# Handing one stage's stream to the next without the trip through memory

## The chip, the cores and the metric

The kernel runs on one core of a Trainium2 chip. The core has five engines that run side by side and wait for each other on semaphores: TensorE (PE, matrix products), VectorE (DVE), ScalarE (ACT), GpSimd (POOL), and SyncE (SP), which issues the transfers here. The metric is the time of one execution in microseconds on the device; lower is better.

## The reference

One transformer block on a stream of 4 x 1024 x 256 float32 values. Modulation vectors come from a small product `c @ wmod` per batch (shift, scale and gate, twice).

1. The stream is normalised over its 256 channels, scaled and shifted; `q`, `k`, `v` are `tanh(x @ W + b)` with 16 heads of 64; causal softmax attention over 1024 tokens; `tanh(ctx @ Wo + bo)`, gated, is added to the stream. Call the sum x1.
2. x1 is normalised again over its channels, scaled and shifted. This feeds two layers. Each has a projection to queries, keys and values of 8 heads on a token-shifted stream, normalised queries and keys with a rotation by position, attention in windows of 128 tokens with one window back, an output product added to the stream, and then a layer norm and a gated GELU feed-forward part, also added.
3. The result is gated and added to x1.

## The kernel before

Tokens lie on the 128 partitions; a batch is 8 tiles of 128 tokens, and the stream of all batches is 32 tiles of 256 channels. Products in float32 accuracy are made of three products of high and low halves (`three_products`, lines 74 to 76), so every operand is split once: the high half by ACT or POOL, the low half as a difference, mostly by DVE. Each engine's program is written out by hand, in order, with counted semaphores; there is no planner.

`phase_modulation_and_attention` works through 4 batches of 8 pairs of heads. A pair (`it`) has 12 units of scores (128 keys by up to 512 queries, for two heads): PE makes scores, ACT takes the exponential (`exps`, L512), DVE splits it (`high_probs` L307, `low_probs` L312), PE multiplies by the values (L710 to L712). In the same pair PE makes the six projections of the next pair (`project`), ACT takes tanh, DVE splits them (`split_projection`, L296), and ACT and DVE split the weights of the pair after that (`split_weights`, L506 and L288). This is done in every pair, in the very last one too, whose next pair does not exist. A batch end follows (PE: L820 to L834): four products of 24 matmuls with `Wo`, each followed by ACT's tanh (L609) and DVE's gate (`gate_attended`, L470), transpositions back, and DVE's addition to the stream (`add_attended`, L477). At the ends of batches 0 and 1 the stream of batch 2 or 3 is also normalised and transposed into `hT`; at the ends of batches 2 and 3 it isn't, there being none. SP stores the sum to x1 in memory (L253) and waits until it has landed.

`phase_layers` is a block of its own: all engines meet before it. SP reads x1 back into `stream` (L1045), then issues the masks, the projection weights `a_raw` (L1050), the rotation tables `rope` (L1052) and their scales, and the layer's other weights. DVE takes statistics of each tile (L1346), the variance in six small steps (`variance_steps`), ACT a square root (L1197) and the normalised tile (L1200), DVE the scale (L1337) and POOL the shift (L1094; DVE for batch 0). Then ACT makes the high half of the projection weights (L1208), DVE multiplies the rotation tables by the scales (L1362) and makes the low half (L1367). PE's first work (`stream_T`, L1597) waits for that.

Then comes a loop over the two layers on every engine (`Fori(0, L)`). A layer begins with a prologue in which the first tiles are transposed, projected and rotated, and goes on with a loop over 32 tiles (attention) and one over 8 chunks (feed-forward). In the attention loop POOL splits the feed-forward weights. In the feed-forward loop it splits the next layer's projection weights (`split_attention_weights`) and then multiplies the rotation tables (L1187). SP reloads these at each layer's end, after the second layer too, for the first one again.

`phase_output` reads x1 once more, gates, adds and stores.

## Time and profile before

| | us |
|---|---|
| median of 3 runs | 2459.71 (2459.40 to 2462.36) |
| the profiled execution's own time | 2460.19 |
| its span, first to last instruction | 2458.4 |
| PE busy | 2292.2 (93%) |
| DVE busy | 1967.5 (80%) |
| ACT busy | 1543.5 (63%) |
| POOL busy | 632.3 (26%) |
| mean granted clock of PE | 0.973 |

### The profile page before, as it was taken

The page shows a single profiled execution, that of the slowest core. Times are in us where ns is not written, and L with a number is a line of the kernel's source. Part 1 is how long each engine was busy: PE and PEld are TensorE (multiplying, and loading weights), DVE is VectorE, ACT ScalarE, POOL GpSimd, SP SyncE. Part 2 cuts the span into 40 slices and gives each one's busy share as a digit, 9 for nine tenths or more (in the row PEclk, how much of TensorE's full clock was granted, in tenths as well). Part 3 has the DMA queues.
Part 4 walks back from the last instruction along what each step waited for, and adds up shares of the span by engine and source line. Part 5 has one row for each costly group of instructions (what it writes and reads, how often), then busy time and mean ns, then how long its engine had stood idle before and what let it go on. Part 6 is the DMA issues. An engine that isn't in the chain of part 4 may idle for free. (4 is left out here: it accounts for less than half of the span.)

```text
span 2458.4 us, 65008 instructions
## 1 busy us (share of the span) xinstructions
PE 2292.2 (93%) x21328; PEld 1759.6 (72%) x21328; DVE 1967.5 (80%) x4616; ACT 1543.5 (63%) x3024; POOL 632.3 (26%) x711
## 2 busy tenths in 40 slices
PE   6999999999999999089999998999899999997995
PEld 4767767777777777067777776888677777776884
DVE  6999799979987996668888887566688888885666
ACT  5777577757765775347677676344477777773442
POOL 1000000000000000245555554222455555552222
PEclk9999999999999999589999999999999999998998
DMA  4000100010001000500000000100100000001004
GB/s 137 20 19 13 59 20 13 29 49 13 13 13 49 13 19 6 186 1 1 9 0 9 0 9 2 53 0 0 47 0 6 2 9 0 9 0 53 0 0 136
DMA packets 70205, 62.44 MB, mean 25 GB/s; under 512 B 3972, under 2 KB 67196, under 8 KB 69760
## 3 DMA queue, kind: packets, MB, share of 16 engines
q1 hardware_dynamic: 70144, 61.66, 7.9%
q8 instruction: 35, 0.57, 0.1%
q14 instruction: 26, 0.21, 0.0%
HBM read 49.05 MB, written 8.40 MB: 23 GB/s over the span
## 5 line engine op out<-in xcount | busy, mean ns | idle before, releaser
L512 ACT ACTIVATE at_p<-at_ps_s,at_shift 128x1024 f32<-128x1024 f32 (+3 forms) x384 | 336.0, 900 | 84.9 <-PE at_ps_s L682 48.6
L312 DVE TENSOR_TENSOR at_p_lo<-at_p,at_p_hi 128x1024 f16<-128x1024 f32 (+3 forms) x384 | 357.2, 951 | 5.5
L1233 ACT ACTIVATE ly_probs<-ly_masked,ly_small,ly_rq 128x256 f32<-128x256 f32 x512 | 301.0, 592 | 9.6 <-DVE ly_small L1426 5.2
L1123 POOL TENSOR_TENSOR ly_rope_a<-ly_rope_a,ly_rope_t 128x512 f32<-128x512 f32 x132 | 168.9, 1279 | 271.4 <-DVE ly_rope_t L1394 271.4
L710 PE MATMUL at_ps_o<-at_v,at_p_hi 128*128 128x65 f16 x2304 | 237.7, 193 | 0.0
L711 PE MATMUL at_ps_o<-at_v,at_p_hi 128*128 128x64 f16 x2304 | 236.8, 194 | 0.0
L712 PE MATMUL at_ps_o<-at_v,at_p_lo 128*128 128x65 f16 x2304 | 235.7, 192 | 0.0
L710 PEld LDWEIGHTS at_ps_o<-at_v,at_p_hi 128*128 128x128 f16 x2304 | 210.6, 96 | 34.5 <-issue 25.8
L307 DVE CAST at_p_hi<-at_p 128x1024 f16<-128x1024 f32 (+3 forms) x384 | 206.7, 556 | 22.7 <-ACT at_p L512 14.2
L1241 ACT ACTIVATE ly_operands_plain<-ly_ps 128x512 f32<-128x512 f32 x256 | 152.5, 596 | 100.8 <-PE ly_ps L1639 100.8
L712 PEld LDWEIGHTS at_ps_o<-at_v,at_p_lo 128*128 128x128 f16 x2304 | 212.3, 99 | 0.0
L711 PEld LDWEIGHTS at_ps_o<-at_v,at_p_hi 128*128 128x128 f16 x2304 | 212.0, 97 | 0.0
L1423 DVE CUSTOM_DVE_ANT_0 ly_masked<-ly_ps,ly_mask 128x256 f32<-128x256 f32 x520 | 199.2, 420 | 5.9 <-PE ly_ps L1628 2.5
L74 PE MATMUL ly_ps<-ly_a_hi,ly_operands 128*128 128x512 f32 x408 | 180.3, 442 | 16.4 <-DVE ly_operands L1373 11.8
L518 ACT ACTIVATE at_stage<-at_ps_m,at_bias 128x512 f32<-128x512 f32 x198 | 135.9, 686 | 77.3 <-PE at_ps_m L76 72.3
L74 PE MATMUL at_ps_m<-at_hT,at_w_hi 128*128 128x512 f32 (+1 forms) x396 | 174.0, 439 | 6.7 <-DVE at_hT L362 3.0
L75 PE MATMUL ly_ps<-ly_a_lo,ly_operands 128*128 128x512 f32 x408 | 163.6, 401 | 0.0
L76 PE MATMUL ly_ps<-ly_a_hi,ly_operands 128*128 128x512 f32 x408 | 162.9, 399 | 0.0
L1639 PE MATMUL ly_ps<-ident,ly_probs 128*128 128x128 f32 x1024 | 161.2, 280 | 0.6
L76 PE MATMUL at_ps_m<-at_hT,at_w_lo 128*128 128x512 f32 (+1 forms) x396 | 157.1, 397 | 0.0
L75 PE MATMUL at_ps_m<-at_hT,at_w_hi 128*128 128x512 f32 (+1 forms) x396 | 156.3, 395 | 0.0
L1649 PE MATMUL ly_ps<-ly_operands_plain,ly_values 128*64 128x128 f32 x2048 | 154.2, 282 | 0.0
(233 smaller groups left out, 6247.7 us busy)
## 6 DMA issues: line engine op xcount, KB each, us to landing
ly_a_raw<-in_ffn_wqkv SPq DMA_DIRECT2D x3, 1536.0 KB, 6.3
at_w_raw<-in_Wv SPq DMA_DIRECT2D x34, 128.0 KB, 2.2
at_w_raw<-in_Wq SPq DMA_DIRECT2D x34, 128.0 KB, 2.3
at_w_raw<-in_Wk SPq DMA_DIRECT2D x34, 128.0 KB, 2.3
at_xio<-in_states SPq DMA_DIRECT2D x4, 1024.0 KB, 6.8
x<-at_xio SPq DMA_DIRECT2D x4, 1024.0 KB, 4.4
stream<-x SPq DMA_DIRECT2D x4, 1024.0 KB, 9.8
out_x<-x SPq DMA_DIRECT2D x4, 1024.0 KB, 9.5
```

What stands on the lines that cost most here:

```text
L74: pe.matmul(out, w_hi, x_hi, start=first, stop=False, skip_group_check=True)
L75: pe.matmul(out, w_hi, x_lo, start=False, stop=False, skip_group_check=True)
L76: return pe.matmul(out, w_lo, x_hi, start=False, stop=last, skip_group_check=True)
L307: dve.tensor_copy(p_hi[u % P_RING][:, :, off:], probs[u % P_RING][:, :, off:]).then_inc(p_hi_done, 1)
L312: dve.tensor_tensor(p_lo[u % P_RING][:, :, off:], probs[u % P_RING][:, :, off:], p_hi[u % P_RING][:, :, off:], ALU.subtract).then_inc(p_lo ...
L512: act.activation(probs[u % P_RING][:, :, off:], ps_s[u % 2][:, :, off:], ACT.Exp, bias=shift[:], scale=SCORE_SCALE).then_inc(exp_done, 1)
L710: pe.matmul(out, ph, ones_hi, start=(kt == 0 and t == 0), stop=False, skip_group_check=True)
L711: pe.matmul(out[:, 0:DH], ph, lo, start=False, stop=False, skip_group_check=True)
L712: step = pe.matmul(out, pl, ones_hi, start=False, stop=(kt == qc * CT + t), skip_group_check=True)
L1123: pool.tensor_tensor(ra[:, i, :], ra[:, i, :], rt[:, i, :], ALU.add).then_inc(s["add_done"], 1)
L1233: step = act.activation(pr[:, j % 2, h, :], sm[:, j % 2, h, :], ACT.Exp, bias=small[:, j % 2, 1, h:h + 1], scale=rq[:, par, 2 * j + h:2 * ...
L1423: dve.tensor_tensor_reduce(sm[:, j % 2, h, :], ps_s[h][:, half], mask[:, par].rearrange("p a b -> p (a b)"), 1.0, -3.0e38, ALU.add, ALU.ma ...
```

## The change

- `stream`, the layers' input, is allocated in the memory of `hT`, the transposed stream of the attention stage. Its first half is `hT`'s half for even batches, free once batch 2's projections are made. The attention stage's query and key buffers share memory with the projection weights `a_raw` and `a_lo`.
- During the attention stage SP reads x1 of batches 0 and 1 back before the end of batch 2, and of batch 2 before the end of batch 3 (`load_attended`). At these batch ends DVE, POOL and ACT do the second norm of those batches with scale and shift (`second_statistics`, `second_shifts`, `second_normal`, `second_scale`, `second_offset`). Batch 3's sum is written straight into `stream` and stored from there; the attention block doesn't wait for that store any more, the layers block does where it writes over it.
- SP issues layer 0's `a_raw` after the last scores of the attention stage.
- Batch 3's norm stands inside layer 0's prologue (`last_statistics`, `last_variance`, `last_shifts`, `last_affine`), ahead of the attention loop. The rotation tables' products (`scale_rotations`) stand behind the first tile's low half. The square root becomes a power on POOL.
- The last pair of the attention stage makes no projections, values, weights or scores for a next one, and the last but one splits no weights.
- The layers are written out one after the other in place of the loop; what the second would prepare for a third is left out (the reload, the split of the projection weights, the rotation tables).

```diff
-        hT = a.sb("at_hT", [P, 2, 2, KT, S], F32R)
+        hT, stream, st_x, a_raw = (keep[n] for n in ("hT", "stream", "st_x1", "a_raw"))
...
+                def load_attended(b):
+                    sp.dma_start(stream[:, b * TB:(b + 1) * TB, :],
+                                 scr["x1"][b].rearrange("(t p) d -> p t d", p=P)).then_inc(ld_s[b], 16)
...
+                    ahead = HP if b + 2 < B else HP - 1 if b + 1 < B else HP - 2
+                    with sp.Fori(0, ahead) as j:
 
                         hold(sp, tick, (wh_done, at(b * HP + j + 2)), (wl_done, at(b * HP + j + 2)))
                         load_w(b * HP + j + 2)
                     if b + 2 < B:
...
+                    elif b + 1 < B:
+                        sp.wait_ge(pj_mm, at(NPJ * HP * (b + 1)))
+                        for i in range(b):
+                            load_attended(i)
+                        sp.wait_ge(wh_done, at(b * HP + HP + 1))
+                        sp.wait_ge(wl_done, at(b * HP + HP + 1))
+                        load_w(b * HP + HP + 1)
+                    else:
+                        sp.wait_ge(pj_mm, at(NPJ * HP * (b + 1)))
+                        load_attended(b - 1)
+                        sp.wait_ge(sc_done, NU * NPAIR)
+                        sp.dma_start(a_raw[:].rearrange("p (k n) -> p k n", k=KT),
+                                     io["ffn_wqkv"][0].rearrange("(k p) n -> p k n", p=P)).then_inc(keep["ld_a"], 16)
 
                     hold(sp, tick, (x1_done, at(NC * (b + 1))))
-                    sp.dma_start(scr["x1"][b].rearrange("(t p) d -> p t d", p=P), xio[:]).then_inc(st_x, 16)
-
-                    hold(sp, tick, (st_x, 16 * b + 16))
+                    src = xio[:] if b + 1 < B else stream[:, b * TB:(b + 1) * TB, :]
+                    sp.dma_start(scr["x1"][b].rearrange("(t p) d -> p t d", p=P), src).then_inc(st_x, 16)
+
+                    if b + 1 < B:
+                        hold(sp, tick, (st_x, 16 * b + 16))
...
+                for b in range(B - 1):
+                    tiles = slice(b * TB, (b + 1) * TB)
+                    pool.wait_ge(n2_var, b + 1)
+                    pool.tensor_tensor(col[:, 2, tiles], col[:, 1, tiles], expo[:], ALU.pow).then_inc(n2_rstd, 1)
...
+                def second_statistics(b):
+
+                    tiles = slice(b * TB, (b + 1) * TB)
+                    dve.wait_ge(ld_s[b], 16)
+                    for t in range(b * TB, (b + 1) * TB):
+                        dve.bn_stats(stats[:, t, :], stream[:, t, :]).then_inc(n2_bn, 1)
+                    dve.wait_ge(n2_bn, TB * (b + 1))
+                    variance_steps(dve, n2_chain, 5 * b, stats[:, tiles], col[:, 0, tiles], vtmp[:, :, tiles], col[:, 1, tiles], n2_var)
+
+                def second_shifts(b):
+                    tiles = slice(b * TB, (b + 1) * TB)
+                    dve.wait_ge(n2_rstd, b + 1)
+                    dve.scalar_tensor_tensor(col[:, 3, tiles], col[:, 0, tiles], -0.5, col[:, 2, tiles], ALU.mult,
+                                             ALU.mult).then_inc(n2_col, 1)
+
+                def second_scale(b):
+                    part = stream[:, b * TB:(b + 1) * TB, :]
+                    dve.wait_ge(st_rows, 16 * (B + 1))
+                    dve.wait_ge(n2_xn, b + 1)
+                    dve.tensor_tensor(part, part, modB[:, b, D:2 * D].unsqueeze(1).broadcast_to([P, TB, D]),
+                                      ALU.mult).then_inc(n2_scaled, 1)
+
+                def second_offset(b):
+                    part = stream[:, b * TB:(b + 1) * TB, :]
+                    dve.wait_ge(n2_scaled, b + 1)
+                    dve.tensor_tensor(part, part, modB[:, b, 0:D].unsqueeze(1).broadcast_to([P, TB, D]),
+                                      ALU.add).then_inc(n2_done, 1)
...
+                        if ahead_of:
+                            split_projection(ahead, 0, dst)
...
+                        if ahead_of > 1:
+                            split_weights(it + 2)
...
+                    with dve.Fori(0, HP // 2 - (0 if b + 1 < B else 1)) as j:
                         for par in range(2):
...
+                            pair(j * 2 + par, par)
+                    if b + 1 == B:
+                        pair(HP - 2, 0, 1)
+                        pair(HP - 1, 1, 0)
...
+                        into = xio[:, tiles, :] if b + 1 < B else stream[:, b * TB + c * CT:b * TB + (c + 1) * CT, :]
+                        dve.tensor_tensor(into, xio[:, tiles, :],
                                           (ps_s[1], ps_o)[c][:].rearrange("p h (t d) -> p (h t) d", d=D), ALU.add).then_inc(x1_done, 1)
 
+                    if b + 2 >= B:
+                        second_statistics(0 if b + 1 < B else b - 1)
+                    if b + 2 == B:
+                        second_statistics(1)
+                        second_shifts(0)
...
+                        second_shifts(1)
+                        second_scale(0)
+                        second_offset(0)
+                        gate_attended(0, 1)
+                        second_scale(1)
+                        gate_attended(1, 0)
+                        add_attended(0)
+                        second_offset(1)
                     else:
+                        second_shifts(b - 1)
+                        second_scale(b - 1)
                         gate_attended(0, 1)
+                        second_offset(b - 1)
...
+                def second_normal(b):
+
+                    act.wait_ge(n2_col, b + 1)
+                    for t in range(b * TB, (b + 1) * TB):
+                        step = act.activation(stream[:, t, :], stream[:, t, :], ACT.Identity, scale=col[:, 2, t:t + 1],
+                                              bias=col[:, 3, t:t + 1])
+                    step.then_inc(n2_xn, 1)
...
+                            if m == 0 and c == 0 and b + 2 >= B:
+                                second_normal(0 if b + 1 < B else b - 1)
+                            if m == 1 and c == 0 and b + 2 == B:
+                                second_normal(1)
...
+                load_attention(0)
+                sp.sem_inc(s["ld_attn"], 16)
                 sp.dma_start(prev_mask[:], io["prev_mask"]).then_inc(s["ld_const"], 16)
                 sp.dma_start(mask[:], io["mask"]).then_inc(s["ld_const"], 16)
...
+                    if l + 1 < L:
+                        hold(sp, s["tick"], (s["qkv_mm"], at(3 * (NT + 2) * (l + 1))))
+                        hold(sp, s["tick"], (s["ra_done"], at(6 * (NT + 1) * (l + 1))))
+                        load_attention(l + 1)
...
+                        pool.wait_ge(n0_var, 1)
+                        pool.tensor_tensor(col0[:, 2, :], col0[:, 1, :], expo[:], ALU.pow).then_inc(n0_rstd, 1)
...
+                        act.wait_ge(n0_col, 1)
+                        act.wait_ge(keep["st_x1"], 16 * B)
+                        for t in range(TB):
+                            step = act.activation(x[:, NT - TB + t, :], x[:, NT - TB + t, :], ACT.Identity,
+                                                  scale=col0[:, 2, t:t + 1], bias=col0[:, 3, t:t + 1])
+                        step.then_inc(n0_xn, 1)
...
+                def last_statistics():
+                    for t in range(TB):
+                        dve.bn_stats(st0[:, t, :], x[:, NT - TB + t, :]).then_inc(n0_bn, 1)
+
+                def last_variance():
+                    dve.wait_ge(n0_bn, TB)
+                    variance_steps(dve, n0_chain, 0, st0, col0[:, 0, :], tmp0, col0[:, 1, :], n0_var)
+
+                def last_shifts():
+                    dve.wait_ge(n0_rstd, 1)
+                    dve.scalar_tensor_tensor(col0[:, 3, :], col0[:, 0, :], -0.5, col0[:, 2, :], ALU.mult, ALU.mult).then_inc(n0_col, 1)
+
+                def last_affine():
+                    sb, cb = (modB[:, B - 1, i * D:(i + 1) * D].unsqueeze(1).broadcast_to([P, TB, D]) for i in range(2))
+                    dve.wait_ge(n0_xn, 1)
+                    dve.tensor_tensor(x[:, last, :], x[:, last, :], cb, ALU.mult).then_inc(n0_scaled, 1)
+                    dve.wait_ge(n0_scaled, 1)
+                    dve.tensor_tensor(x[:, last, :], x[:, last, :], sb, ALU.add).then_inc(n0_done, 1)
+
+                def scale_rotations():
+                    dve.wait_ge(s["ld_attn"], 48)
+                    for i in range(4):
+                        dve.tensor_tensor(rope[:, i], rope[:, i], rows[:, i, :].unsqueeze(1).broadcast_to([P, TB, DH]),
+                                          ALU.mult).then_inc(s["rope_q"], 1)
+                    after(dve, "rope_q", 4)
...
-                with dve.Fori(0, L) as l:
+                for l in range(L):
                     after(dve, "f_lo", nth_norm(l, 0))
                     stream_lo(l, 0, 0)
                     after(dve, "rope_next", 4 * l)
+                    if l == 0:
+                        scale_rotations()
+                        last_statistics()
                     squared_norms(l, 0, 1)
                     squared_norms(l, 0, 0)
                     rotate_q(l, 0, 0)
                     stream_lo(l, 1, 1)
+                    if l == 0:
+                        last_variance()
                     normalise_keys(l, 0)
                     rotate_k(l, 0, 0)
+                    if l == 0:
+                        last_shifts()
                     squared_norms(l, 1, 1)
                     copy_keys(l, 0, 0)
                     squared_norms(l, 1, 0)
                     stream_lo(l, 2, 0)
+                    if l == 0:
+                        dve.wait_ge(s["ld_const"], 32)
                     after(dve, "msk", (NT // 2 + 1) * l)
                     dve.tensor_copy(mask[:, 0, 1, :], prev_mask[:, 0, :]).then_inc(s["msk"], 1)
                     after(dve, "msk", (NT // 2 + 1) * l + 1)
                     maxima(l, 0, nth(l, 0), 0, 0)
                     maxima(l, 0, nth(l, 0), 1, 0)
+                    if l == 0:
+                        last_affine()
...
+        keep["stream"] = a.sb("stream", [P, NT, D])
+        with ExitStack() as shared:
+            keep["qk"] = [Allocator(nc, shared).sb(f"at_{n}{part}", [P, S], F16)
+                          for n in ("q0", "k0", "q1") for part in ("hi", "lo")]
+        with ExitStack() as shared:
+            keep["a_lo"] = Allocator(nc, shared).sb("ly_a_lo", [P, KT * 3 * INNER], F32R)
+        keep["a_raw"] = a.sb("ly_a_raw", [P, KT * 3 * INNER])
         phase_modulation_and_attention(nc, io, scr, keep)
-        keep["stream"] = a.sb("stream", [P, NT, D])
...
```

## Rows read from the trace of the kernel before

**Rows 1.** The page, 40 equal slices of the span: busy tenths of PE and DVE.
```profile
PE   6999999999999999089999998999899999997995
...
DVE  6999799979987996668888887566688888885666
```

**Rows 2.** Table of stretches: start:end, length, busy us (instructions) by engine, PEclk, DMA, GB/s.
```profile
939.20:965.20 26.00, 25.02 (x358) 18.02 (x357) 24.71 (x38) 19.09 (x27) 0.00 (x0) 1.00 0.04 11
...
990.00:1000.00 10.00, 0.07 (x1) 0.00 (x0) 1.22 (x1) 1.28 (x1) 1.17 (x7) 0.69 0.52 173
...
1030.00:1050.00 20.00, 0.68 (x2) 0.29 (x2) 15.29 (x7) 5.75 (x8) 12.00 (x7) 0.50 0.00 1
...
1048.00:1076.00 28.00, 19.48 (x73) 13.82 (x71) 13.97 (x37) 9.12 (x22) 13.16 (x16) 0.75 0.00 1
```

**Rows 3.** Timeline of the hand-over: start, us busy, engine, line, operation [idle before <-releaser].
```profile
990.11 1.22 DVE L477 TENSOR_TENSOR at_xio<-at_xio,at_ps_o 128x1024 f32<-128x1024 f32 x1 [1.19 <-PE at_ps_o L729]
991.42 0.37 SPq L253 DMA_DIRECT2D x<-at_xio  x1
996.33 5.73 SPq L1045 DMA_DIRECT2D stream<-x  x4
...
998.16 0.52 POOL L1089 MEMSET ly_values<- 128x512 f32 x1
1002.07 2.71 DVE L1346 BATCH_NORM_STATS2 ly_masked<-stream 128x6 f32<-128x256 f32 x8 [10.75 <-DMA stream<-x]
...
1005.39 0.17 DVE L89 SCALAR_TENSOR_TENSOR ly_masked<-ly_masked 128x8 f32<-128x8 f32 x1
...
1010.76 2.28 DVE L1337 TENSOR_TENSOR stream<-stream,modB 128x2048 f32<-128x2048 f32 x1
1010.88 4.04 ACT L1200 ACTIVATE stream<-stream,ly_masked 128x256 f32<-128x256 f32 x8 [0.47 <-DVE ly_masked L1352]
...
1031.59 2.84 ACT L1208 ACTIVATE ly_a_hi<-ly_a_raw 128x1536 fp32r<-128x1536 f32 x2
1031.71 4.84 DVE L1337 TENSOR_TENSOR stream<-stream,modB 128x2048 f32<-128x2048 f32 x1 [1.91 <-ACT stream L1200]
1036.47 6.99 DVE L1362 TENSOR_TENSOR ly_rope<-ly_rope,ly_rows 128x512 f32<-128x512 f32 x4
...
1043.39 3.62 DVE L1367 TENSOR_TENSOR ly_a_lo<-ly_a_raw,ly_a_hi 128x1536 fp32r<-128x1536 f32 x2
...
1047.70 0.68 PE L1597 MATMUL ly_ps<-ident,ly_xs 128*128 128x128 f32 x2 [57.64 <-DVE ly_a_lo L1367]
1048.66 1.28 ACT L1214 ACT_TABLE_LOAD   x1 [14.23 <-PE ly_ps L1597]
```

**Rows 4.** Timeline of the block change from the layers to the output, DVE and SP.
```profile
2430.08 1.29 DVE L1584 TENSOR_TENSOR stream<-stream,ly_ps 128x512 f32 x2 [0.54 <-PE ly_ps L1704]
...
2431.64 5.43 SPq L852 DMA_DIRECT2D out_x<-x  x4
```

**Rows 5.** DVE's timeline in the last pair.
```profile
943.40 1.28 DVE L296 TENSOR_TENSOR at_vT_lo<-at_stage,at_vT_hi 128x512 f16<-128x512 f32 x2
...
962.49 0.95 DVE L288 TENSOR_TENSOR at_w_lo<-at_w_raw,at_w_hi 128x768 fp32r<-128x768 f32 x1
```

**Rows 6.** DVE's timeline at the end of batch 2: the first two gates.
```profile
736.07 0.49 DVE L470 TENSOR_SCALAR at_y<-at_y,modT 128x512 f32<-128x512 f32 x1 [5.54 <-ACT at_y L609]
741.67 0.49 DVE L470 TENSOR_SCALAR at_y<-at_y,modT 128x512 f32<-128x512 f32 x1 [5.11 <-ACT at_y L609]
```

**Rows 7.** Timeline of layer 0's prologue and the first tile of its loop.
```profile
1064.15 1.28 POOL L1123 TENSOR_TENSOR ly_rope_a<-ly_rope_a,ly_rope_t 128x512 f32<-128x512 f32 x1 [0.46 <-DVE ly_rope_t L1394]
...
1068.04 1.65 POOL L1119 TENSOR_TENSOR ly_rk<-ly_norm,ly_expo 128x8 f32<-128x8 f32 x1 [2.61 <-DVE ly_norm L1382]
...
1072.75 0.69 DVE L1391 TENSOR_TENSOR ly_rope_a<-ly_ps,ly_rope 128x512 f32<-128x512 f32 x1
...
1078.56 0.48 PE L74 MATMUL ly_ps<-ly_a_hi,ly_operands 128*128 128x512 f32 x1
```

More of the change, by code:

```diff
@@ L604, in _ @@
+                    with act.Fori(0, HP // 2 - (0 if b + 1 < B else 1)) as j:
+                        for par in range(2):
+                            pair(j * 2 + par, par)
+                    if b + 1 == B:
+                        pair(HP - 2, 0, 1)
+                        pair(HP - 1, 1, 0)
                     for c in range(NC):
@@ L1144, in split_attention_weights @@
                     pool.tensor_tensor(a_lo[:, cols], a_raw[:, cols], f32(a_hi[:, cols]), ALU.subtract).then_inc(s["aw_done"], 1)
-                with pool.Fori(0, L) as l:
+                for l in range(L):
                     hold(pool, s["tick"], (s["ya_done"], at(NCH * l)))
@@ L1273, in u_high @@
                     act.activation(uT[rows_of, 0, i, :], uf[rows_of, i % 2, :], ACT.Copy).then_inc(s["u_hi"], 1)
-                with act.Fori(0, L) as l:
+                for l in range(L):
                     after(act, "y_mm", HT * NCH * l)
@@ L1712, in _ @@
                 after(pe, "w_lo_done", 2)
-                with pe.Fori(0, L) as l:
+                for l in range(L):
                     after(pe, "ya_done", NCH * l)
```

356 lines of the change are left out of this document (174 added, 182 removed).

## The prediction

> **What bounds the kernel now.** I read the page first: the slices of TensorE (PE) read nine almost everywhere, and zero in one, the seventeenth [rows 1]. That slice is where the attention stage hands over to the layers. The table of stretches gives its size: from 990 to 1000 us PE does one instruction, from 1030 to 1050 two, while VectorE (DVE) is busy 15.3 of 20 us, and the granted clock has fallen from 1.00 to 0.50 [rows 2]. So the kernel is bound by PE in its steady parts and by a chain of other engines in this gap. The timeline then gives that chain [rows 3]. DVE's last addition of the attention stage runs from 990.11 to 991.33. The result is stored (issue at 991.42), and the stream is read back by four transfers from 996.33. Statistics begin at 1002.07. For each of four batches DVE, ScalarE (ACT) and GpSimd (POOL) normalise, scale and shift in turn, and after that come the rotation tables (1036.47) and the low half of the projection weights (1043.39 to 1047.01). PE starts at 1047.70. From 991.33 to 1047.70 are 56.4 us with no matmul. Nothing else in the kernel is a bubble of this kind, apart from the last stage, which the change leaves as it is.
>
> **The change, part by part.** The sum is made against the profiled execution: span 2458.4 us, its own time 2460.2 us, which is 0.5 above the median 2459.7 of the runs shown.
>
> *The gap.* In the new kernel batches 0 to 2 arrive normalised, batch 3 is normalised later, the projection weights are in place, and the attention block no longer waits for its last store. What stays between DVE's last addition and PE's first transposition is:
> - the block change. Where nothing is stored it is short: the layers' last addition ends at 2431.37 and the next block's first transfer is issued at 2431.64 [rows 4]. I take 0.6 us, since the store's issue (0.37) now stands before SP's end: the new block starts at 991.9.
> - the start. The block began by 996.25 and POOL's last memset ended at 998.68 [rows 3], so 2.4 us: 994.3. A table load of ACT (1.28) fits under it.
> - the high half of the weights on ACT, 2.84 for two pieces, and behind its second piece one low half on DVE, 1.8 (half of 3.62) [rows 3]: 994.3 + 2.84 + 1.8 = 998.9, and 0.1 for the waits.
> PE therefore starts at 999.0 instead of 1047.7: **-48.7 us**. Bounds: -50.0 if the block starts at once and the pieces overlap better, -44 if the weights or the block end wait for something (the old wait for the store, 4.4 us, is the largest that stood here).
> The weight load is issued after the last scores, some 35 us before the end of the stage, into their memory. It is not on the path. The rotation tables are: they land behind the last store (1 MB) and are wanted only after the first low half of the stream, about 2 us after PE's start, 9 us after their issue. I take no wait, with 3 us as the upper bound.
>
> *The last pair without a next one.* The pairs are held by DVE, busy 24.7 of 26 us in the last one [rows 2]. The last pair drops six splits of projections (0.64 each, 1.28 for two), one copy of values of about the same size (0.6) and the split of weights (0.95, which overlaps to 0.86) [rows 5]: 5.3 us of DVE. PE, busy 25.0 of the 26, drops the 36 matmuls of six projections and more, and ACT, busy 19.1, drops twelve tanh, so neither takes over. Not all of it comes back, because at the end of the pair the context must pass PE and ACT before DVE can take its low half, and this stood behind the dropped split. I take **-4.5 us**, between -2 (PE and ACT latencies laid bare) and -6.6 (all of DVE's dropped work in both last pairs and its idle time).
>
> *Second norms inside the batch ends.* At a batch end without a next stream PE has four products of 24 matmuls, 5.6 us apart, and DVE idles for 5.5 and 5.1 us before its first two gates [rows 6]. Per batch come 2.71 (statistics), 0.74 (variance), and 2.28 twice (scale and shift); ACT gets 4.04, POOL a power of 1.65 [rows 3, 7]. At the end of batch 2 two batches are done. From DVE's end of the pairs on: statistics to 6.9, first shift column 7.1, gate 7.5, ACT's normals 7.2 to 11.3, scale and offset to 15.9, second gate 16.4. The first gate began 5.54 after DVE's pairs had ended (730.5), and the next 5.6 later [rows 6]; so the third product is done about 16.0 after that end, and there PE wants the second gate. That is **+0.5 us** (0 to +2). At the end of batch 3 only one batch is done, and its second gate comes at 13.2: nothing.
>
> *Layer 0's prologue.* It gains DVE work: four products of the rotation tables, 0.7 each where POOL is quiet (6.99 for four with POOL busy), statistics 2.71, variance 0.74, and before the loop the two operations on batch 3 (4.57). The first two fall before ACT's first square, about 7 us after DVE's first low half, and are hidden. The variance sits before the keys are normalised, +0.7. POOL's power of 1.65 comes before the second addition of the rotated keys, which began at 1064.15 [rows 7]: with the 0.7 it starts at 1065.4 on the old scale, +1.3 for everything behind. Then ACT normalises eight tiles (4.04), DVE scales and shifts: DVE's first rotation of the loop moves from 1072.75 to 1078.9. PE is not that late: its second projection of the loop, which waits for the keys, moves from 1078.56 to 1081.0 [rows 7]. From there on all is shifted by **+2.4 us**. Bounds: 0 if the steady part, where DVE's slices read eight [rows 1], gives it back, and +9.6 (0.7 + 1.65 + 4.04 + 2.28 and 0.9 for the clock, which read 0.75 in this stretch [rows 2]) if it stands on the path in full.
> The Trainium skill speaks against this step (SBUF — State Buffer, the section "SBUF: two separate sides"): DVE and GpSimd share a port pair as an exclusive lock, held for a whole instruction. The trace agrees: DVE's product on a whole batch took 2.28 us alone and 4.84 beside POOL's addition [rows 3]. By that rule the two operations before the loop would cost up to 5 us more, a sum of 2413.6. I leave it out because POOL here waits for them and has only short work.
>
> *The table load.* ACT loads a table at 1048.66, on the path between PE's first transposition and the copy of it, after the square root earlier in the block [rows 3]. The change computes no square root there: **-1.3 us** (0 if the load stays).
>
> *Layers unrolled; the reload at the end dropped.* The matmuls, waits and shapes inside the loops are the same. The second layer's useless weight split and its four products on POOL go, beside a PE whose slices read nine [rows 1]: 0. Waits whose value depended on the layer become constants: 0, bounds -3 to +3, since PE's slices read nine with that register work in its program.
>
> Sum: -48.7 - 4.5 + 0.5 + 2.4 - 1.3 = -51.6, so 2460.2 - 51.6 = 2408.6 us.
>
> **The rivals.**
> - *The prologue pays in full.* The work taken out of the gap comes back behind PE's restart: DVE's products wait for the tables (+3), its operations run beside POOL's, the power, normals and scaling stand on the path, and PE goes in and out of half clock as it does in this stretch now [rows 2]. For it: DVE is the busiest engine there, and its first operation of the loop does move by 6 us. Against: PE needs only the keys' part of it. Time: 2460.2 - 48.7 - 3 + 1 + 9.6 + 1 = 2420.
> - *More comes back.* The last pair gives all of DVE's dropped work (-6.6), the prologue costs nothing since the loop has slack, the register work shrinks (-3): 2460.2 - 50 - 6.6 - 1.3 - 1 = 2401.
> - *The other side: slower code in the unrolled layers.* The layers are now laid out twice, with new wait values and fresh code for the second layer at every loop entry. If a tile of the layers' attention (about 14 us, 64 of them) became 0.9 us longer, that is 58 us, and the kernel would end above 2465. It takes the whole gain back from 0.8 us a tile (51.6 / 64). For it: PE has no slack in that part. Against: the operations are the same, and the first layer's fresh code does not show as idle time in the slices now [rows 1].
> - *The gap stays in part:* the attention block ends late, since the last store or the weights hold it. 4.4 us: 2413. It is inside the range.
>
> **How the numbers follow.** Forecast 2408.5, chance 0.70 (2404 to 2414). Prologue in full 0.13, more comes back 0.13, slower code 0.02, and 0.02 for anything that holds the layers' start for nearly as long as now. The range that leaves out 2 in 10 is 2401 to 2419. A measurement of this kernel tells 0.2% (5 us) from nothing; all cases but the last two are far beyond it: faster 0.96, same 0.015, slower 0.025.
>
> **What would show it.** PE's idle stretch at the hand-over falls from 56.4 to about 8 us; the last pair lasts about 21.5 us instead of 26; PE's second projection of layer 0's loop begins about 32 us after its first transposition (30.9 now); no table load after that transposition; the stretches of the layers' loops are as long as now. The forecast is wrong if the gap is above 15 us, if a tile in the layers takes more than 14.3 us, or if DVE's two operations on batch 3 hold PE for more than 5 us.

## The result and the profile after

The changed kernel takes 2426.3 us (median of 4 runs, 2423.5 to 2427.0) against 2460.4 (median of 4, 2459.4 to 2462.4): a ratio of 0.9855, 95% interval 0.9843 to 0.9867. That is 34 us less, where 51 were forecast, and outside the range (2401 to 2419). The gap closed as forecast, and most of what is missing was lost in a place that the prediction had put at 0: in layer 1's attention loop ACT loads a table in every iteration.

I cut the spans at marks that both kernels have: the issues of the four stores of x1, PE's first transposition of the layers, and each layer's first and last addition of attended values on DVE. Times in us; the further columns are experiments told below.

| from, to | before | changed | exp once | last pair only | additions on DVE | all |
|---|---|---|---|---|---|---|
| start, first store | 285.38 | 286.96 | 286.60 | 286.49 | 285.56 | 285.73 |
| batch 1 | 236.67 | 237.20 | 237.19 | 236.76 | 237.17 | 237.17 |
| batch 2 | 235.07 | 235.60 | 235.55 | 235.25 | 235.60 | 235.60 |
| batch 3 | 234.29 | 231.45 | 231.43 | 229.38 | 229.85 | 229.84 |
| last store, PE's restart | 56.29 | 8.31 | 8.31 | 55.85 | 8.31 | 5.36 |
| restart, first addition | 30.89 | 31.79 | 31.61 | 30.34 | 31.75 | 33.53 |
| layer 0's loop | 450.73 | 449.70 | 449.75 | 450.99 | 449.73 | 450.96 |
| to layer 1's first addition | 241.18 | 238.05 | 237.85 | 241.23 | 237.97 | 237.99 |
| layer 1's loop | 450.72 | **466.88** | 450.30 | 450.98 | 450.24 | 450.25 |
| to the end | 237.16 | 239.25 | 236.01 | 236.62 | 235.67 | 235.62 |
| span | 2458.39 | 2425.18 | 2404.59 | 2453.89 | 2401.84 | 2402.04 |

The page of the changed kernel, the slices of PE and DVE. The zero of [rows 1], the seventeenth, is now a six. Nothing here betrays the loss in layer 1 (the 29th to the 36th slice): an engine that waits 1 us in 29 doesn't move a tenth.

```profile
PE   6999999999999999699999997999899999998994
...
DVE  6999799979998998688888886666788888885666
```

The table of stretches around the hand-over answers to [rows 2] (start:end, length, busy us and instructions by engine, PEclk, DMA share, GB/s). The first row covers the last pair. From DVE's last context product of the pair before (L352) to its own last one it now takes 23.6 us, against 26.1 in the kernel before; its granted clock is no longer 1.00.

```profile
941.00:965.00 24.00, 18.30 (x303) 12.35 (x302) 20.01 (x31) 11.61 (x15) 0.00 (x0) 0.93 0.21 78
...
990.00:1000.00 10.00, 0.49 (x2) 0.29 (x2) 4.54 (x3) 2.85 (x2) 2.95 (x12) 0.62 0.75 222
1000.00:1020.00 20.00, 15.29 (x57) 11.21 (x56) 14.75 (x38) 5.44 (x14) 11.31 (x11) 0.76 0.47 172
```

The timeline of the hand-over answers to [rows 3]. Read it as one chain: the last addition ends at 991.11, the store is issued, the new block's first transfer comes at 992.00, POOL's last memset ends at 994.36, ACT starts its high halves behind it, DVE's two low halves run one after the other to 999.41, and PE transposes at 999.51. ACT's copy of that comes without a table load.

```profile
989.89 1.22 DVE L547 TENSOR_TENSOR stream<-at_xio,at_ps_o 128x1024 f32<-128x1024 f32 x1 [1.19 <-PE at_ps_o L848]
991.20 0.37 SPq L276 DMA_DIRECT2D x<-stream  x1
992.00 0.35 SPq L1181 DMA_DIRECT2D ly_rope<-in_rope  x1
...
993.84 0.52 POOL L1222 MEMSET ly_values<- 128x512 f32 x1
994.39 2.85 ACT L1330 ACTIVATE ly_a_hi<-ly_a_raw 128x1536 fp32r<-128x1536 f32 x2 [6.21 <-POOL ly_values L1222]
...
995.98 3.43 DVE L1491 TENSOR_TENSOR ly_a_lo<-ly_a_raw,ly_a_hi 128x1536 fp32r<-128x1536 f32 x2 [4.87 <-ACT ly_a_hi L1330]
...
999.51 0.66 PE L1731 MATMUL ly_ps<-ident,ly_xs 128*128 128x128 f32 x2 [9.65 <-DVE ly_a_lo L1491]
1000.35 0.28 ACT L1336 ACTIVATE ly_operands<-ly_ps 128x128 fp32r<-128x128 f32 x1 [3.11 <-issue]
```

Now the lost part. ACT's groups by line name the table loads of the whole changed kernel: 16 of them stand at L1355, the exponential inside the attention loop.

```profile
L1355 ACT ACT_TABLE_LOAD x16 | 20.5, 1283 | 3.3 <-DVE ly_small L1549 2.4 <-issue 0.7
...
L1439 ACT ACT_TABLE_LOAD x2 | 2.6, 1283 | 5.9 <-PE ly_ps L1800 5.9
...
L649 ACT ACT_TABLE_LOAD x1 | 1.3, 1283 | 1.3 <-PEq L1993 1.3
```

The same view of the kernel before has six loads in all, none in a loop over tiles; two of them are at the first copy of a layer:

```profile
L1214 ACT ACT_TABLE_LOAD x2 | 2.6, 1283 | 19.4 <-PE ly_ps L1597 19.4
```

ACT's timeline at the head of one iteration in layer 1: the load, and 0.02 us after it the exponential that needed it. The next is at 1801.62, 29.3 us on, and so through the loop; an iteration is two tiles.

```profile
1771.72 0.60 ACT L1367 ACTIVATE ly_operands_plain<-ly_ps 128x512 f32<-128x512 f32 x1 [2.19 <-PE ly_ps L1793]
1772.33 1.28 ACT L1355 ACT_TABLE_LOAD   x1
1773.63 0.60 ACT L1355 ACTIVATE ly_probs<-ly_masked,ly_small,ly_rq 128x256 f32<-128x256 f32 x1
```

And PE's waits (us in total, times, longest). First layer 1's loop in the changed kernel, 1719 to 2186, then layer 0's, 1031 to 1481, where the exponential's table is still active from the attention stage and nothing is loaded. In the kernel before, PE waits in layer 1's loop (1771 to 2221) only once, for 1.6 us.

```profile
PE ly_ps L1773 <- ACT ly_probs L1355: 15.7, 15, 1.2
PE ly_ps L1800 <- DVE ly_operands_plain L1565: 1.6, 1, 1.6
```

```profile
PE ly_ps L1800 <- DVE ly_operands_plain L1565: 1.6, 1, 1.6
PE ly_ps L1773 <- ACT ly_operands_plain L1363: 0.2, 1, 0.2
```

This is how I read it. A load is placed where an instruction needs a table that may not be active. In the rolled loop over the layers the first copy of a layer got one, since the code before it can be the entry or the previous layer's Gelu, and the exponential loop inherited it. Unrolled, the prologue of layer 1 holds only copies and squares, which run under Gelu's table, so nothing is loaded there; the loop's first exponential is reached with Gelu's table at the entry and with its own from the loop's end, and gets a load that runs every time.

### The profile page after: what moved, and what is told of

Read it like the earlier page. It is cut to its first block and busy times, and to the rows that moved or that the text cites. A ratio compares the mean times of both kernels' runs of the same rounds, so it can differ in the third digit from the quotient of the medians.

```text
span 2425.2 us, 63570 instructions
## 1 busy us (share of the span) xinstructions
PE 2288.2 (94%) x21268; PEld 1753.3 (72%) x21268; DVE 1957.4 (81%) x4606; ACT 1551.4 (64%) x3018; POOL 604.0 (25%) x692
## 5 line engine op out<-in xcount | busy, mean ns | idle before, releaser
L1355 ACT ACTIVATE ly_probs<-ly_masked,ly_small,ly_rq 128x256 f32<-128x256 f32 x512 | 301.4, 594 | 2.6 <-DVE ly_small L1549 1.4
L829 PE MATMUL at_ps_o<-at_v,at_p_hi 128*128 128x64 f16 x2304 | 237.2, 194 | 0.0
L335 DVE CAST at_p_hi<-at_p 128x1024 f16<-128x1024 f32 (+3 forms) x384 | 206.5, 556 | 25.8 <-ACT at_p L599 14.3
L74 PE MATMUL at_ps_m<-at_hT,at_w_hi 128*128 128x512 f32 (+1 forms) x384 | 169.2, 441 | 5.9 <-DVE at_hT L390 3.0
L1773 PEld LDWEIGHTS ly_ps<-ident,ly_probs 128*128 128x128 f32 x1024 | 117.6, 140 | 64.5 <-issue 49.4
L75 PE MATMUL at_ps_m<-at_hT,at_w_hi 128*128 128x512 f32 (+1 forms) x384 | 152.7, 398 | 0.0
```

What stands on the lines that cost most here:

```text
L74: pe.matmul(out, w_hi, x_hi, start=first, stop=False, skip_group_check=True)
L75: pe.matmul(out, w_hi, x_lo, start=False, stop=False, skip_group_check=True)
L335: dve.tensor_copy(p_hi[u % P_RING][:, :, off:], probs[u % P_RING][:, :, off:]).then_inc(p_hi_done, 1)
L829: pe.matmul(out[:, 0:DH], ph, lo, start=False, stop=False, skip_group_check=True)
L1355: step = act.activation(pr[:, j % 2, h, :], sm[:, j % 2, h, :], ACT.Exp, bias=small[:, j % 2, 1, h:h + 1], scale=rq[:, par, 2 * j + h:2 * ...
L1773: step = pe.transpose(ps_pt[:, (2 * slot + h) * P:(2 * slot + h + 1) * P], pr[:, j % 2, h, slot * P:(slot + 1) * P], ident[:])
```

## The experiments

Theory A: these loads are the loss. Theory B: the second copy of the layers' code is slow by itself, and the loads hide in ACT's idle time. The first three runs tell them apart. Each ratio is to the kernel before, run again in the same round: it took 2461.2 us beside the first four experiments, 2462.0 beside the next four and 2461.4 beside the last two, so times of different rounds can differ by some 0.8 us for that alone.

**The exponential once, ahead of layer 1 (the base of what follows).**

```diff
+        warm_exp = a.sb("ly_warm_exp", [P, 1])
...
                 for l in range(L):
+                    if l:
+                        act.activation(warm_exp[:], expo[:, 0:1], ACT.Exp)
                     after(act, "y_mm", HT * NCH * l)
```

> The changed kernel with one more instruction: an exponential of one column on ACT at the head of layer 1, ahead of ACT's first wait there, so that the table of the exponential is active before layer 1's attention loop begins. Theory A (the loss is the table loads inside the loop: in the changed kernel's trace 16 loads of 1.28 us stand ahead of L1355 in layer 1's loop, one each 29.3 us, and PE waits 15 times for ACT's copy of the probabilities, 15.7 us in all): layer 1's attention loop goes from 466.9 back to about 451 us (450.7 before), loads in the trace 5 instead of 19, the time 2426.3 - 15.7 = 2410 (2408 to 2412). Theory B (the second copy of the layer's code or its constant waits make it slow, the loads fall into ACT's idle time): layer 1's loop stays above 464, the time 2424 to 2428.

Measured: 2407.5 us (5 runs, 2404.1 to 2410.6), ratio to before 0.9782 (0.9769 to 0.9795). Its four loads are at 1.27, 1480.54, 1685.27 and 2168.68, layer 1's loop is back at 450.30, and of PE's waits in it one is left:

```profile
PE ly_ps L1803 <- DVE ly_operands_plain L1568: 1.6, 1, 1.6
```

One instruction more gives 19 us in the medians. The two profiled executions differ by 20.6: 16.8 of it are the loop and the stretch before it (466.88 to 450.30, 238.05 to 237.85), 1.05 for each of 16 loads; 3.2 are at the end of the kernel and have another cause, which this instruction doesn't touch (below). Theory B falls. I had counted five loads; there are four.

**Only the unrolling, in the kernel before.**

```diff
-                with act.Fori(0, L) as l:
+                for l in range(L):
```

(the same on the other four engines)

> The kernel before with one part of the change alone: the loop over the layers is laid out twice on all five engines, nothing else. Here the table that is active at the entry of layer 0's attention loop is the square root's, so by theory A both layers' loops get a load in each of their 16 iterations: 32 loads at about 1.03 us each (15.7 / 15 as PE waited in layer 1 of the changed kernel), less the two loads at the head of the layers (1.3 each at most): 2460.4 + 33 - 2 = 2491 (2486 to 2495), each layer's loop 16 us longer than 450.7. Theory B (second copy of the code alone): only layer 1's loop is longer, 2476. My prediction's own term for this part was 0 (2457 to 2463).

Measured: 2489.6 us (4 runs, 2486.2 to 2492.6), ratio 1.011 (1.0095 to 1.0125). Both loops are longer, 467.09 and 466.88, and all 32 iterations load:

```profile
L1233 ACT ACT_TABLE_LOAD x32 | 41.1, 1283 | 6.7 <-DVE ly_small L1426 4.8 <-issue 1.5
```

So this part of the change, alone, makes the kernel 28 us slower. What it gives back is also seen: without the load at layer 1's head the stretch between the loops falls from 241.18 to 239.19.

**A Gelu ahead of layer 0, in the changed kernel.**

```diff
+        warm_gelu = a.sb("ly_warm_gelu", [P, 1])
...
                 for l in range(L):
+                    if l == 0:
+                        act.activation(warm_gelu[:], expo[:, 0:1], ACT.Gelu)
                     after(act, "y_mm", HT * NCH * l)
```

> The changed kernel with one more instruction: a Gelu of one column on ACT at the head of layer 0, so that the exponential's table is no longer active when layer 0's attention loop begins. Theory A: layer 0's loop gets 16 loads as layer 1's has and goes from 449.7 to 466 us; one more load of 1.28 us stands ahead of the first copy of the stream, beside the hand-over: 2426.3 + 16.2 + 0 to 1.3 = 2443 (2441 to 2445). Theory B: layer 0's loop stays at 450 and the time at 2426 to 2428.

Measured: 2441.3 us (4 runs, 2438.6 to 2443.8), ratio 0.9915 (0.99 to 0.993). Layer 0's loop, untouched, goes from 449.70 to 466.46, and PE waits there as it does in layer 1:

```profile
PE ly_ps L1776 <- ACT ly_probs L1356: 16.0, 15, 1.3
```

The table that is active when a loop is entered decides, not which copy of the code it is.

**Only the last pair, in the kernel before.** The edit is the change's `pair` with `ahead_of` on DVE, ACT and PE, and SP's two weight loads fewer.

> The kernel before with one part of the change alone: the last two pairs of the last batch laid out by themselves, the last without a next one and the one before without a split of weights (DVE, ACT and PE drop six projections' work, the copy of values and the split of weights). My prediction had -4.5 us for it (-2 to -6.6): 2455.9. What the changed kernel's trace shows: from the third to the fourth store of the attention stage 231.4 us instead of 234.3, so -2.9 with both pairs, and in the last pair PE's granted clock at 0.70 in 945 to 950 us with DVE waiting 1.81 us for PE. If those 2.9 are this part's whole effect, 2457.5 (2457 to 2458). If the batch end of the change had hidden a part of it, 2455.9. The rest of the kernel, layers included, is as before.

Measured: 2456.3 us (11 runs, 2453.2 to 2461.7), ratio 0.9984 (0.9975 to 0.9993), and batch 3 is 4.9 us shorter (234.29 to 229.38). Alone the part gives what was forecast, in the changed kernel only 2.8. The stretch 940 to 950 shows where the larger part went: PE's idle gaps there are the same in both kernels (1.06, 0.29 and 0.52 us, waiting for ACT and DVE), but in the changed kernel, first fence, the granted clock is 0.83 over the stretch, that is at its lower level for 3.4 us of it, while in the last pair alone, second fence, it stays at 1.00.

```profile
940.00:950.00 10.00, 8.12 (x107) 4.41 (x107) 7.52 (x14) 5.67 (x7) 0.00 (x0) 0.83 0.19 66
```

```profile
940.00:950.00 10.00, 7.98 (x136) 4.94 (x136) 9.36 (x16) 6.38 (x8) 0.00 (x0) 1.00 0.00 2
```

DVE does less in the first (7.52 against 9.36 us): it waits once for PE, 1.8 us. So far this is a coincidence of two things in two traces; the next two experiments bear on it.

**Seven unread matmuls in those gaps, in the base.**

```diff
+                    def unread_products(it, par, n):
+                        pe.wait_ge(ct_lo, at(NC * it - 1))
+                        for _ in range(n):
+                            pe.matmul(ps_m[0][:], qk[par][0][0][:, 0:P], qk[par][0][0][:, 0:CH], start=True, stop=True,
+                                      skip_group_check=True)
...
                         if ahead_of:
                             project(it, 0, buf)
+                        else:
+                            unread_products(it, par, 5)
                         scores(b, it, par, 2, 3)
                         if ahead_of:
                             project(it, 1, buf)
+                        else:
+                            unread_products(it, par, 2)
```

> The base with seven additional matmuls in the last pair of the attention stage, whose results nobody reads: five of 128x512 f16 ahead of the scores of units 2 and 3 (PE idle there for 1.06 us, waiting for ACT) and two ahead of the first value products (0.52, waiting for DVE). In the three traces with the whole change these gaps are followed by 3.4 us of half clock (0.88 and 0.78 or 0.96 and 0.70 in the stretches from 940 and 945), in the last pair alone the same gaps are not, and batch 3 lasts 231.4 us (store to store) in the former and 229.4 in the latter. Theory A (the half clock takes the 2 us, and it follows from the gaps): the clock reads 1.00 throughout the pair, batch 3 lasts 229.5 us, time 2405.5. Theory B (the 2 us come from the transfers of the batches' streams and weights into memory beside the pair, or from the second norms): batch 3 stays at 231.4, time 2407.5 to 2408.

Measured: 2407.0 us (5 runs, 2404.4 to 2409.9), ratio 0.9777 (0.9763 to 0.9791), not told apart from the base. The profiled execution lost elsewhere (restart to first addition 32.34, to the end 239.18), so its total can't show 1.6 us in the pair. In its trace the clock is 1.00 and batch 3 lasts 229.85:

```profile
940.00:950.00 10.00, 8.85 (x136) 4.97 (x133) 9.07 (x16) 7.54 (x9) 0.00 (x0) 1.00 0.15 51
```

**The last stage's additions all on DVE, in the base.** The stretch to the end was 3 us longer in the changed kernel than in the base (239.25, 236.01), which no term had.

```diff
-POOL_BATCHES = (1,)
+POOL_BATCHES = ()
```

> The changed kernel with the exponential at the head of layer 1 (the first experiment, 2407.5 us, called the base here), and the last stage's four additions all on DVE instead of three there and one on POOL. In the traces POOL's addition and DVE's first one become ready within 0.3 us of each other: where DVE was first (kernel before, base, last pair alone) the first output store is issued 221 us after layer 1's last attended addition and the span ends at 236.0 to 237.2; where POOL was first (changed kernel, Gelu first, unrolled alone) the store is at 224 to 225 and the end at 238.2 to 239.3. Theory A (the two share something, and who comes first decides 3 us): without POOL four additions of 2.28 us follow each other, the last store is issued at about 227.6 instead of 229.3 after that mark, the end at 234.3, the time 2405.8. Theory B (the output is bound by the transfers): end at 236, no change, 2407.5.

Measured: 2404.8 us (5 runs, 2403.7 to 2406.1). It isn't told apart from the base: the intervals of the ratios, 0.9758 to 0.9784 and 0.9769 to 0.9795 for the base, overlap. The timelines tell the cause. In the changed kernel, first fence, POOL begins 0.23 us ahead of DVE, takes 4.67 us, and DVE's first addition isn't over before 2411.07 (three take 10.98; the first output store is issued at 2411.10). In the base, second fence, DVE is first: its addition takes 2.28, POOL's 6.57, and the first store is issued at 2389.16, 2.3 us after DVE's start.

```profile
2404.26 4.67 POOL L1015 TENSOR_TENSOR stream<-stream,out_x 128x2048 f32<-128x2048 f32 x1 [28.61 <-DMA out_x<-x]
2404.49 10.98 DVE L1007 TENSOR_TENSOR stream<-stream,out_x 128x2048 f32<-128x2048 f32 x3
```

```profile
2386.84 2.28 DVE L1007 TENSOR_TENSOR stream<-stream,out_x 128x2048 f32<-128x2048 f32 x1
2386.91 6.57 POOL L1015 TENSOR_TENSOR stream<-stream,out_x 128x2048 f32<-128x2048 f32 x1 [28.91 <-DMA out_x<-x]
```

With all four on DVE they take 8.89 us and there is no race:

```profile
2384.45 8.89 DVE L1007 TENSOR_TENSOR stream<-stream,out_x 128x2048 f32<-128x2048 f32 x4
```

Whoever comes first runs at full speed and the other waits it out. The Trainium skill has this rule for two additions as these (SBUF — State Buffer, the section "SBUF: two separate sides"): whichever of the two starts first keeps the shared port pair for its whole instruction. The trace agrees: in the base POOL ends 4.36 us behind the end of DVE's 2.28, near the 4.67 that it takes when it is first; in the changed kernel DVE ends 2.14 us behind POOL's end. In the kernel before, POOL's record begins 0.04 us ahead of DVE's and yet DVE took its 2.29 us and POOL 6.68, so who was first can't be read from starts that lie so close. The stretch to the end fell less than expected, to 235.67 and not 234.3. Counted from layer 1's last attended addition, the last store is issued 2.1 us earlier than in the base (227.2 against 229.3), but the four stores of 1 MB land 2.7 us apart (at 227.1, 229.8, 232.6 and 235.3), later than the additions would need: the transfers set the end there.

This run also corrects the pair's story. Its attention stage is the base's, and yet its clock stayed at 1.00 and batch 3 lasted 229.85. So the gaps don't bring the lower clock by necessity. The same code with and without the lower clock also gives its price: 231.43 against 229.85 us.

**An earlier start at the hand-over, in the base.**

```diff
-                start(act, ACT_SEMS)
-
-                act.wait_ge(s["zeroed"], B + 2)
                 act.wait_ge(keep["ld_a"], 16)
...
+                start(act, ACT_SEMS)
+                act.wait_ge(s["zeroed"], B + 2)
...
-                after(pe, "w_lo_done", 2)
                 for l in range(L):
                     after(pe, "ya_done", NCH * l)
                     stream_T(l, 0, 0)
+                    if l == 0:
+                        after(pe, "w_lo_done", 2)
```

(and DVE's wait for the memsets behind its low halves)

> The base with the hand-over's chain rearranged: ACT's high half of the projection weights ahead of its semaphore credits and of its wait for POOL's memsets, DVE's low half ahead of the same wait, and PE's first transposition no longer behind the low half (only the first projection waits for it). In the base ACT's first copy began at 993.96 behind POOL's last memset, DVE's low halves ran from 995.55 to 998.98, PE's first transposition came at 999.08, 8.3 us after the last store's issue. Theory A (the 8.3 us are this chain, what my prediction called start and weights): ACT starts at 991.6, DVE's low halves run from 993.8 (the end of its own credits) to 997.3, the transposition comes at 994.6 and the first projection as soon as the low half is there: layer 0's first attended addition 1.7 to 3.3 us earlier counted from the last store, time 2404.2 to 2405.8. Theory B (layer 0's prologue waits for DVE and POOL work, rotations first, not for PE's start): 0 to 0.5 us, 2407.

Measured: 2406.7 us (5 runs, 2404.5 to 2412.2), ratio 0.9779 (0.9763 to 0.9795), not told apart from the base; the profiled execution had POOL first at the end (239.22). PE restarts after 5.35 us instead of 8.31, its first projection comes 2.3 us earlier, but the first attended addition only 1.1. DVE, next, waits for the rotation tables' scales to land:

```profile
1000.05 1.90 DVE L1485 TENSOR_TENSOR ly_rope<-ly_rope,ly_rows 128x512 f32<-128x512 f32 x3 [1.92 <-DMA ly_rows<-in_qk_rows]
```

**Layer 0's prologue without the last batch's norm, in the base.**

```diff
                     if l == 0:
                         scale_rotations()
-                        last_statistics()
...
-                    if l == 0:
-                        last_affine()
```

(likewise the variance, POOL's power, the shifts, ACT's normals, and the waits that belong to them, the one for the last store of x1 among them; the last batch enters the layers without its second norm, so this kernel computes something else)

> The base without the last batch's second normalisation in layer 0's prologue (statistics, variance, POOL's power, shifts, ACT's eight normals, DVE's scale and offset; the wait for the last store goes with them): the last batch enters the layers as it is. The rotation tables' four products stay. My prediction gave the prologue +2.4 us, nearly all of it from the variance and the power ahead of the rotated keys' second addition. Base: 31.6 us from the first transposition to the first attended addition, against 30.9 before, of which a table load of 1.3 stood only in the kernel before. Theory A (the norm is what costs): 29.5 us, time 2405.3. Theory B (the rotation tables' products and the waits on them cost it, the norm is hidden): 31.3 us, time 2407.2.

Measured: 2406.2 us (4 runs, 2405.3 to 2406.7), ratio 0.9774 (0.976 to 0.9789), not told apart from the base. The prologue falls from 31.61 to 29.16, that is by 2.45 us, as theory A has it; layer 0's loop then takes 450.34 instead of 449.75, all of the difference in its first tile (14.12 against 13.49), so 1.9 us stay. The stretch to layer 1's first addition is 1.0 us shorter than in the base as well (236.86), for which I have no cause. This execution had POOL first at the end (238.66), so its total does not show the gain.

**All of it together, with and without the unread matmuls.**

> The version that the runs point to: the exponential at the head of layer 1, the last stage's additions all on DVE, the rearranged hand-over, and the seven unread matmuls in the last pair. From parts: additions on DVE 2404.8, less the 1.1 us that the rearranged hand-over gave between the last store and layer 0's first attended addition (38.82 against 39.92), less 0 to 1.6 for the last pair (the half clock there was in five of six traces without the unread matmuls and not in the one with them): 2403.0 (2402 to 2404). If the parts are not independent: 2405 to 2406.

> The same without the seven unread matmuls. Theory A (they keep the clock up): its trace shows half clock in the last pair in most executions, batch 3 lasts 231.4 us, and the median is 1 to 2 us above the version with them: 2404.0 to 2405. Theory B (whether the clock falls there is a matter of when the execution reaches the gaps, and the matmuls change nothing): the two medians agree within 0.5 us.

Measured: 2404.2 us with them (5 runs, 2403.9 to 2405.4, ratio 0.9772, 0.9758 to 0.9785) and 2405.5 without (5 runs, 2403.5 to 2406.4, ratio 0.9772, 0.9759 to 0.9786). 2404.2 lies between the two times expected for it. 2405.5 is 1.3 above it, which is what theory A had, but the runs of the two overlap, so they aren't told apart. Batch 3 lasts 229.84 and 231.44. The earlier start is given back in both: the loop of layer 0 takes 1.2 us more (450.96) than in the base, all of it in the first tile (14.72 against 13.49). The early start by itself does not bring this, since in its own experiment the loop took 449.69; what does is open. So the version with the additions on DVE alone is as good, within the interval, and all three beat both the kernel before and the changed one.

## Why the prediction was wrong, step by step

*The step that failed* is "Layers unrolled; the reload at the end dropped", put at 0 because "the matmuls, waits and shapes inside the loops are the same", together with "The table load", -1.3. These are indeed the same, but a table load is none of the three. The load at layer 0's head did go, as forecast, and so did the one at layer 1's head, which I had not counted. In their place 16 stand in layer 1's loop: +16.2 us (450.72 to 466.88); of a load's 1.28 us, 1.05 stand on PE's path. The unrolled kernel by itself shows it without the rest of the change, the exponential ahead of the loop takes it away. My rival "slower code in the unrolled layers" had the place but the wrong mechanism and no bound from a load per iteration: 1.28 for 16 or 32 iterations is 20 to 41 us, which would have stood in the range if I had asked which table is active at the loop's head.

*The gap.* -48.7 forecast, -48.0 measured (56.29 to 8.31). From DVE's last addition to PE's restart are 8.4 us where I had 7.7. ACT started 3.3 us behind that addition (3.0 forecast; 994.39 looks nearer to my 994.3 than it is, since the addition ended 0.2 us earlier than before). The rest is in the halves: DVE's two low halves ran in sequence behind ACT's first, 5.0 us in all where I had 4.64.

*The last pair.* -4.5 forecast; -4.9 alone, -2.8 in the changed kernel. The size was right; about 1.6 of it went to the lower clock (231.45 against 229.85 us in the same code with and without it), and the other 0.5 is what batches 1 and 2 are longer too. The pair itself lasts 23.6 us, and 22.1 in the last pair alone, where my mark was 21.5.

*Batch 2's end.* +0.5 forecast. The batch is 0.53 longer, but so is batch 1, where nothing was added to the end. From DVE's last work on the pairs (ends at 733.17) to the store's issue (759.76) are 26.6 us as before: the norms cost nothing there. The 0.5 in each of batches 1 and 2 sits in the pairs, some 0.06 each, and I did not find its cause.

*The prologue.* +2.4, of which the norm's removal gave back 2.45. With the table load that left, +1.1 was forecast from PE's restart and +0.9 measured. The mark I named reads otherwise: PE's second projection came 30.8 us after the first transposition, not 32, so up to there the prologue cost 1.2 and not 2.4. 0.6 us more come back in the first tile of the loop (13.49 against 14.10). DVE's two operations on batch 3, for whose meeting with POOL I left out up to 5 us, took 2.29 us each: POOL was idle beside them (6.60 us, waiting for them).

*Not forecast.* +1.6 up to the first store, which is no loss of the change: this stretch reads 286.07 and 286.49 in the two variants of the kernel before, and 285.56 to 286.95 in the other traces with the change. -1.0 in layer 0's loop, 0.6 in its first tile and the rest at its three changes of batch (14.14 against 14.27 us). -3.1 between the loops, of which 1.3 is layer 1's table load and 2.0 came with the unrolling alone (the load within it); the other 1.1 is unexplained. +2.1 at the end, from POOL coming first.

*Sums of the rivals.* "More comes back" names -3 for the register work but adds -1; with -3 it would be 2399, outside the range, which began at 2401. "The prologue pays in full" adds -3, +1 and +1 without a name for them; with the terms of the main sum and the +3 for the tables it would be 2460.2 - 48.7 - 4.5 + 0.5 + 9.6 - 1.3 + 3 = 2418.8, not 2420. Neither would have put 2426.3 into the range.

Of the signs that I had named for a wrong forecast one came: a tile above 14.3 us (466.88 for 32 is 14.6).

Taken together, the base, which has all parts of the change and no load in a loop, runs in 2407.5 us, where the sum was 2408.6. The nearness is partly luck: the 1.6 us missing in the last pair and the gap's missing 0.7 stand against the -3.1 between the loops that no term had, and whether DVE or POOL comes first at the end moves it by as much again.

## What to carry to other kernels

When a loop is unrolled or a block reordered, ask for each inner loop which activation table is active at its entry and at its end; if the two can differ, the load runs in every iteration. One tiny activation ahead of the loop settles it. The term for the slice in which PE stood still came out within 0.7 us of its sum of rows (-48.0 for -48.7). The term that failed is the one without a sum: "the same instructions" must include those that nobody wrote.

## What the runs showed of the hardware

- A table load takes 1.28 us and the next activation starts 0.02 us later. The Trainium skill gives the same 1283 ns (ScalarE: Activation LUTs, the section "What ACT_TABLE_LOAD costs") and adds some 1.4 us of drain for a switch. No drain is seen here: in the loop the load also begins 0.01 us behind the activation before it, and it cost 1.05 us of the kernel's time.
- The same code can meet the lower clock or not. With the changed attention stage and no unread matmuls, six of seven traces have it in the last pair and one doesn't; with the unread matmuls none of two has. Two traces are too few to call it shown that the matmuls prevent it, and the medians (2404.2 and 2405.5; 2407.0 and 2407.5) don't settle it.
- Two large additions, one on DVE and one on POOL, that become ready within 0.3 us of each other make the end of the kernel longer or shorter by which of them runs first. With the changed kernel's last stage it is 236.0 us with DVE first (one trace) and 238.7 to 239.3 with POOL first (five traces); in the kernel before and its variants 236.6 and 237.2 against 238.2.
